# Layer 1's prologue written out on its own: decay and keys of batch 0 ahead of its gate, whose projection moves into the first period

## The reference

```
xa = layernorm(x); sx = previous row of xa - xa
t  = tanh((xa + sx * maa_x) @ maa_w1);  mw, mk, mv, mr, mg = t_f @ maa_w2[f]
x? = xa + sx * (maa_? + m?)                       for ? in w, k, v, r, g
w  = exp(-exp(time_decay + tanh(xw @ decay_w1) @ decay_w2))
r, k, v = xr @ Wr.T, xk @ Wk.T, xv @ Wv.T;   g = silu(xg @ Wg.T)
for each row l:  a = k_l v_l^T;  out_l = r_l (faaaa * a + s);  s = a + w_l * s
x = x + (groupnorm(out) * g) @ Wo.T;  then a gated feed-forward block on layernorm(x)
```

## Time and profile before

| what | us |
| --- | --- |
| median of 3 runs | 3539.14 |
| profiled execution, its time | 3535.91 |
| profiled execution, first to last instruction (span) | 3534.1 |
| layer 1, from its first instruction to its last unit, in the trace | 1400.87 to 2249.4 |
| first scan starts | 1470.82 |
| mean granted clock of TensorE, share of full | 0.968 |

### The profile page before, as it was taken

The page is one execution under the profiler, slowest core; times in us unless marked ns, Lnnn a source line. Parts: engine busy times, 40 slices in busy tenths (PEclk is TensorE's granted clock), DMA queues, the critical chain, the costliest instruction groups (busy, mean ns, idle before and its releaser), DMA issues. The chain is left out here.

```text
span 3534.1 us, 55156 instructions
## 1 busy us (share of the span) xinstructions
PE 3319.9 (94%) x21472; PEld 2547.0 (72%) x21472; DVE 2390.6 (68%) x3781; ACT 1787.9 (51%) x4255; POOL 196.2 (6%) x311
## 2 busy tenths in 40 slices
PE   7999999999999997889999998679999999699998
PEld 6777888887777785656666665357788788488885
DVE  6666666666665665499999999637777887642213
ACT  4555444444454443456565554427777777532222
POOL 0000000000000000000000000001111111000000
PEclk9999999999999999899999999879999999899999
DMA  5332212231122211544444444120001110210004
GB/s 215 124 105 107 108 72 76 97 115 72 72 96 90 78 73 57 156 114 103 111 108 102 114 103 108 41 108 3 35 31 70 44 48 31 88 53 24 24 12 162
DMA packets 93456, 296.08 MB, mean 84 GB/s; under 512 B 20016, under 2 KB 28208, under 8 KB 68752
## 3 DMA queue, kind: packets, MB, share of 16 engines
q1 hardware_dynamic: 64896, 186.47, 18.0%
q0 software_dynamic: 10368, 75.50, 5.6%
q10 hardware_dynamic: 17936, 30.59, 2.5%
HBM read 233.82 MB, written 58.72 MB: 83 GB/s over the span
## 5 line engine op out<-in xcount | busy, mean ns | idle before, releaser
L537 ACT ACTIVATE l_prob<-l_bank,l_nmax 128x512 f32<-128x512 f32 x512 | 345.3, 687 | 276.8 <-DVE l_nmax L679 276.8
L679 DVE TENSOR_REDUCE l_nmax<-l_bank 128x1 f32<-128x512 f32 x512 | 317.5, 682 | 71.4 <-PE l_bank L409 71.2
L375 PE MATMUL l_bank<-l_x_hi,l_w_hi 128*128 128x256 f32 x1024 | 298.0, 291 | 11.7 <-DVE l_x_lo L779 11.7
L702 DVE COPY l_probT<-l_bank 128x512 f32<-128x512 f32 x256 | 173.7, 689 | 175.3 <-PE l_bank L423 173.2
L375 PE MATMUL l_bank<-l_x_hi,l_w_lo 128*128 128x256 f32 x1024 | 290.9, 284 | 0.0
L375 PE MATMUL l_bank<-l_x_lo,l_w_hi 128*128 128x256 f32 x1024 | 290.7, 284 | 0.0
L1752 DVE TENSOR_TENSOR_SCAN l_kv<-l_wx,l_kv 128x2056 f32<-128x2056 f32 x64 | 283.8, 4434 | 1.6 <-DVE first_nrs L1765 1.2
L2320 ACT ACTIVATE l2a_sc<-l2a_sc,l2a_nmax 128x256 f32<-128x256 f32 x512 | 254.8, 508 | 41.1 <-DVE l2a_nmax L2436 41.1
L423 PE MATMUL l_bank<-l_ident,l_prob 128*128 128x128 f32 x2048 | 247.9, 275 | 10.7 <-DVE l_k_lo L695 6.3
L423 PEld LDWEIGHTS l_bank<-l_ident,l_prob 128*128 128x128 f32 x2048 | 225.8, 141 | 24.4 <-DVE l_k_lo L695 16.3
L445 PE MATMUL l_bank<-l_probT,l_v 128*64 128x512 f32 x1024 | 233.8, 598 | 0.0
(11 more groups left out here) (353 smaller groups left out, 8207.5 us busy)
## 6 DMA issues: line engine op xcount, KB each, us to landing
l_vb<-vd SPq DMA_DIRECT2D x64, 1024.0 KB
l_w_hi<-kept_w_hi POOLq DMA_DIRECT2D x24, 1024.0 KB, 8.2
l_w_lo<-kept_w_lo POOLq DMA_DIRECT2D x24, 1024.0 KB, 10.2
l_wv_hi<-kept_wv_hi POOLq DMA_DIRECT2D x12, 1024.0 KB, 5.1
l_wv_lo<-kept_wv_lo POOLq DMA_DIRECT2D x12, 1024.0 KB, 7.1
kept_w_hi<-l_w_hi SPq DMA_DIRECT2D x8, 1024.0 KB, 8.8
kept_w_lo<-l_w_lo SPq DMA_DIRECT2D x8, 1024.0 KB, 11.2
l2a_x<-x SPq DMA_DIRECT2D x16, 512.0 KB, 3.8
```

The source lines that it names most:

```text
L375: mm = pe.matmul(s.ap[:, c * ROWS:(c + 1) * ROWS], a[:, kt, c, g, :], b[:, kt, c * ROWS:(c + 1) * ROWS], start=m == 0, stop=m == 3 * KT - 1)
L537: act.activation(prob[h][:, it, :], s.ap[:, :], ACT.Exp, bias=nmax[:, n % 2, it, h:h + 1], accum_out=rsum[:, n % 2, it, h:h + 1]).then_inc ...
L679: dve.tensor_reduce(nmax[:, n % 2, it, h:h + 1], s.ap[:, :], AX.X, ALU.max, negate=True).then_inc(max_ready, 1)
L702: dve.tensor_copy(probT[0][:, j, :], s.ap[:, :]).then_inc(s.drained, 1)
```

## The change

The prologue is taken out of the loop (`ALL` is now `range(B + 1)`, POOL alone keeps its pass b = -1) and written out for each engine. Its order is new: mixtures v, w, g; centre_rows(1); project v; decay_in; mixture k; column_variances(1); decay_out; mixture r; project k half 0; spread_deviations(1); project r half 0. Project g of batch 0 stands in the first period, between centre_rows(2) and project v of batch 1. Inputs of batch 0 take other buffers: x, w, r in `xf[0]`, v and k in `xf[1]`, g in `ig[0]`. Since `xf[0]` now holds the input of r, `first_part(1)` waits until r half 1 of batch 0 is projected. `Wg` is loaded behind `Wk` and `Wr`.

```diff
@@ the list of PSUM tiles
-    ALL = range(-1, B + 1)
+    ALL = range(B + 1)
+    FIRST_INPUTS = ["x", "v", "w", "g", "k", "r"]
...
-    ring = []
+    ring = ["xT0_0", "xT0_1", "t0", "mv0_0", "mv0_1", "mw0_0", "mw0_1", "mg0_0", "mg0_1", "nc1_0", "nc1_1", "v0_0", "v0_1", "d0",
+            "mk0_0", "mk0_1", "nv1", "w0_0", "w0_1", "mr0_0", "mr0_1", "k0_0", "nr1", "r0_0"]
...
-        ring += [f"o{c}_0", f"o{c}_1"] if c is not None else []
+        ring += [f"o{c}_0", f"o{c}_1"] if c is not None else ["g0_0", "g0_1"]
...
+        def input_of(p, n):
...
+            if p == 0:
+                return {"x": xf[0], "v": xf[1], "w": xf[0], "g": ig[0], "k": xf[1], "r": xf[0]}[n]
+            return xf[INPUTS.index(n) % 2]
@@ SyncE
-                for n in ("Wv", "Wg"):
-                    sp.dma_start(W[n][:, :, :], d["l1_" + n]).then_inc(W_in[n], 16)
+                sp.dma_start(W["Wv"][:, :, :], d["l1_Wv"]).then_inc(W_in["Wv"], 16)
                 sp.dma_start(dw1[:, :, :], d["l1_dw1"]).then_inc(dw1_in, 16)
-                for n in ("Wk", "Wr"):
+                for n in ("Wk", "Wr", "Wg"):
@@ TensorE
+                turn("xT0", x)
+                pe.wait_ge(first_in, 32)
+                pe.wait_ge(w2_in, 48)
+                first(0)
+                mixture(0, "v")
+                mixture(0, "w")
+                mixture(0, "g")
+                centre_rows(1)
+                project(0, "v")
+                decay_in(0)
+                mixture(0, "k")
+                column_variances(1)
+                decay_out(0)
+                mixture(0, "r")
+                project(0, "k", (0,))
+                spread_deviations(1)
+                project(0, "r", (0,))
                 for b in ALL:
...
                         rows(f"o{c}", y, W["Wo"])
+                    else:
+                        project(0, "g")
                     if 0 <= p < B:
                         project(p, "v")
@@ ScalarE
                     if p:
                         full(act, S[f"k{p - 1}_1"])
+                    if p == 1:
+                        full(act, S["r0_1"])
...
+                turned(0)
+                first_part(0)
+                tanh(0)
+                mixture(0, "v")
+                mixture(0, "w")
+                mixture(0, "g")
+                centred(1)
+                for half in H2:
+                    project(0, "v", half, iv)
+                store_v(0)
+                decay_in(0)
+                mixture(0, "k")
+                decay_out(0)
+                mixture(0, "r")
+                project(0, "k", 0, ik)
+                start_state(0)
+                spread_w(0, 0)
+                stats(1)
                 for b in ALL:
...
                         spread_w(b, 2)
                     if c >= 0:
                         stats_c(c)
+                    else:
+                        full(act, S["g0_1"])
+                        for half in H2:
+                            project(0, "g", half, ig[0], ACT.Silu)
                     if now:
                         start_state(PER * b + 4)
@@ VectorE
+                shift(0)
+                first_input(0)
+                mix(0, "v")
+                mix(0, "w")
+                mix(0, "g")
+                column_deviations(1)
+                mix(0, "k")
+                mix(0, "r")
+                scale_rows(1)
+                spread(0)
                 for b in ALL:
```

More of the change, by code:

```diff
@@ L1025, in input_count @@
         def input_count(p, n):
-            return len(INPUTS) * p + INPUTS.index(n) + 1
+            return len(INPUTS) * p + (INPUTS if p else FIRST_INPUTS).index(n) + 1
+        def input_of(p, n):
+            if p == 0:
+                return {"x": xf[0], "v": xf[1], "w": xf[0], "g": ig[0], "k": xf[1], "r": xf[0]}[n]
+            return xf[INPUTS.index(n) % 2]
         def halves(ap):
@@ L1123, in _ @@
                 pool.memset(wx[:, :, 0], 0.0).then_inc(wx_zeroed, 1)
-                for b in ALL:
+                for b in range(-1, B + 1):
                     if b >= 1:
@@ L1219, in project @@
                     pe.wait_ge(xf_ready, input_count(p, n))
-                    columns(f"{n}{p}", W["W" + n], xf[INPUTS.index(n) % 2], own)
+                    columns(f"{n}{p}", W["W" + n], input_of(p, n), own)
                 def decay_in(p):
@@ L1228, in decay_in @@
                     for kt in range(CT):
-                        mm = pe.matmul(s.ap[0:64, 0:ROWS], dw1[:, kt, :], xf[1][:, kt, :], start=kt == 0, stop=kt == CT - 1)
+                        mm = pe.matmul(s.ap[0:64, 0:ROWS], dw1[:, kt, :], input_of(p, "w")[:, kt, :], start=kt == 0, stop=kt == CT - 1)
                     mm.then_inc(s.full, 1)
@@ L1302, in _ @@
                     if 0 <= p < B:
-                        if p:
-                            pe.wait_ge(xn_ready, p)
+                        pe.wait_ge(xn_ready, p)
                         turn(f"xT{p}", x)
@@ L1315, in _ @@
                     if 0 <= p < B:
-                        if p == 0:
-                            pe.wait_ge(first_in, 32)
-                            pe.wait_ge(w2_in, 48)
                         first(p)
@@ L1499, in mixture @@
                 def mixture(p, n):
-                    i = INPUTS.index(n)
+                    to = input_of(p, n)
                     if n == "v" and p:
                         full(act, S[f"r{p - 1}_1"])
-                    if n != "v":
+                    if n != "v" and p:
                         full(act, S[{"g": f"t{p}", "w": f"v{p}_1", "k": f"g{p}_1", "r": f"d{p}"}[n]])
+                    if n in "wkr" and p == 0:
+                        full(act, S[{"w": "t0", "k": "v0_1", "r": "d0"}[n]])
                     for half in H2:
@@ L1509, in mixture @@
                             m = M0 + MIX.index(n)
-                            ins = act.activation(xf[i % 2][:, ct, :], s.ap[:, ct % 2 * ROWS:(ct % 2 + 1) * ROWS], ACT.Identity,
+                            ins = act.activation(to[:, ct, :], s.ap[:, ct % 2 * ROWS:(ct % 2 + 1) * ROWS], ACT.Identity,
                                                  bias=vec[:, m, ct:ct + 1])
@@ L1792, in mix @@
                 def mix(p, n):
-                    i = INPUTS.index(n)
-                    to = xf[i % 2]
+                    to = input_of(p, n)
                     for half in H2:
@@ L1797, in mix @@
                     dve.tensor_tensor(to[:, :, :], to[:, :, :], sx[:, :, :], ALU.mult).then_inc(xf_part, 1)
-                    dve.wait_ge(xf_part, (len(INPUTS) - 1) * p + i)
+                    dve.wait_ge(xf_part, input_count(p, n) - 1 - p)
                     dve.tensor_tensor(to[:, :, :], to[:, :, :], xa[:, :, 1:ROWS + 1], ALU.add).then_inc(xf_ready, 1)
@@ L1895, in _ @@
                             gate_input(c)
-                        if 0 <= unit + 1 and b < B:
+                        if b < B:
                             spread(unit + 1)
```

## The result

| | before | after |
| --- | --- | --- |
| median, 20 runs each | 3536.15 us | 3548.59 us |
| lowest to highest | 3528.23 to 3546.00 | 3541.39 to 3554.56 |
| profiled execution's span | 3534.1 | 3549.3 |

The change makes the kernel slower: ratio 1.0031, 95% interval 1.0024 to 1.0038, 12.4 us by the medians. The forecast was 9.8 us. It named 3549 us and the median is 3548.59, but so near a hit is partly luck: its base, the median of 3 runs, was 3539.14, which is 3.0 above the median of 20.

The account below looks back on a forecast made before the run. The prediction took VectorE, 98% busy from the first unit on, to bound the kernel. To the median of 3539.14 us it added +1.0 (prologue) and +8.8 (first period), +9.8 in all, for 3549 us, range 3538 to 3558.

Parts of the forecast that it names:

- VectorE sets the pace behind the first unit: Layer 1, periods 1 to 8: VectorE is 98% busy, so each microsecond of earlier delay delays the kernel by one.
- The first scan hangs on x1_ready through SyncE's queue: End of prologue: the first value transfer, behind the store of x1, sets the first scan; it takes 14.68 us.
- Rival (b): First scan starts when keys and decay are ready, not held by x1_ready: -4.6 us, 3534.5; chance 0.05.
- Part 1: Prologue: TensorE's new order moves x1_ready and so the first scan by +1.0 us, bounds -1.4 and +4.0.
- Part 2: First period: first_part(1) on ScalarE waits for r half 1, so VectorE is 2.4 us late at first_input(1).
- Part 3: First period: project g delays the variances, VectorE waits 4.7 us, then again at scale_rows(2); +8.8 with Part 2.
- the second term: First period: VectorE's further wait at scale_rows(2), started at 1535.82, now 1544.64; 1.7 us.
- (a): First period: project g is hidden, only the wait of first_part(1) is paid: +3.4 us, 3542.5; chance 0.10.
- (c): Prologue and first period: 1.2 GHz over project k and project g or v: +14.5 us, 3553.6; chance 0.21.
- the bound of 10.6 us: Whole kernel: a change within 0.3%, 10.6 us, counts as no change; the forecast sum was just under it.

Follow-up runs that it names:

- a4: Changed kernel with SyncE's two first value loads ahead of store_x1(1) and load_att(2): 3534.55 us against 3537.05 for the kernel before, ratio 0.9992.
- b1: Kernel before with SyncE's two first value loads ahead of store_x1(1) and load_att(2): 3531.51 us, ratio 0.9985 to the kernel before.
- c1: Kernel before, unchanged, profiled once more: one execution, 3545.38 us.
- c3: Changed kernel, unchanged, profiled a second time: one execution, 3547.76 us.
- a2: Changed kernel with the input of r of batch 0 in tile y, so no wait of first_part(1): 3543.62 us, ratio 1.0016 to the kernel before.
- a3: Changed kernel with project g of batch 0 ahead of picks(0) and the input of r in y: 3538.27 us, ratio 0.9997 to the kernel before.
- a1: Changed kernel with project g of batch 0 moved into TensorE's idle time ahead of picks(0): 3541.86 us against 3539.19 before, ratio 1.0008.
- c2: Kernel before, unchanged, profiled a third time: one execution, 3545.84 us.
- a5: Changed kernel with project g of batch 0 ahead of picks(0), input of r in y, two value loads first: 3529.73 us, ratio 0.9984 to the kernel before.
- a7: Changed kernel with value loads first, input of r in y, project g of batch 0 ahead of picks(6): 3524.43 us against 3537.97 before, ratio 0.9961.
- b2: Kernel before with only the wait of first_part(1) for r half 1 of batch 0 added: 3543.92 us against 3537.05, ratio 1.0019.
- a6: Changed kernel with the 16 products of k half 1 of batch 0 done four times over: 3542.47 us, ratio 1.0013 to the kernel before.

## Why the prediction was right, and where its terms were off

**VectorE sets the pace behind the first unit: right.** Every delay of the first period was kept to the end of the layer: 681.8 us from unit 8 to the last scan against 680.9.

**The first scan hangs on x1_ready through SyncE's queue: right, and shown by a4 and b1.** Its transfer left 1.0 us behind scale_rows(1), as before. Rival (b), an early first scan, needed SyncE's order to change; with that order changed (a4) the gain is there.

**Part 1, +1.0: off.** In the pair of profiles it was +0.1 for x1_ready and -0.2 for the first spread. Two errors nearly cancel. From start to start decay_out took 1.99 us, mixture r 3.70 and half of k 4.99: by the prediction's own sum that is 1.99 + 3.70 + 4.99 - 8.79 = +1.89. Against it stands the mixture that moved ahead of project v, for which the prediction allowed some 2 us there. Before, mixtures v and g took 3.65 us together; after, v, w and g took 3.86. TensorE before, then after:

```profile
1419.84 1.99 PE L1212 MATMUL l_bank<-l_tT,l_w2a 32*128 32x256 f32 x8 [0.86 <-ACT l_tT L1495]
1421.67 1.88 PE L1212 MATMUL l_bank<-l_tT,l_w2b 32*128 32x256 f32 x8
```
```profile
1418.54 2.31 PE L1219 MATMUL l_bank<-l_tT,l_w2a 32*128 32x256 f32 x13 [0.86 <-ACT l_tT L1519]
...
1420.69 0.37 PE L1219 MATMUL l_bank<-l_tT,l_w2a 32*128 32x256 f32 x1
1420.81 0.37 PE L1219 MATMUL l_bank<-l_tT,l_w2b 32*128 32x256 f32 x1
```

Mixture w contracts rows 0 to 31 of its tiles, v and g rows 64 to 95. Products of w and g appear in turn, 0.11 us from start to start; products of one and the same mixture start 0.24 us apart. So mixture w came nearly free, 0.2 us for 1.9. Together that is +1.89 - 1.71 = +0.2, and spread_deviations(1) came 0.2 us later in the layer than before.

Against the five profiles of the old prologue the new one is some 3 us early (first spread at 67.0 to 68.9 in six profiles, 67.5 to 74.2 in four of the old). I had one profile, of an execution with little of the slow clock in its prologue. Read by half microseconds, the granted clock falls to 1.2 GHz at 20.6 us from the layer's start in the other four of the old prologue, during the first mixture, and is back at 27.5 (30.3 in c1). In the first profile of before and in all nine with the new prologue it stays at 2.4 GHz from 17.5 to 33 us. (My theory for c1, that the clock rises at one of two moments, is not what these rows show: it has risen by 17.5 us in all of them.) Up to the second mixture TensorE does the same in both prologues, so that their order of mixtures is not what keeps the clock up. Whether another part of the change does, or the nine had luck, is not settled.

**Part 2, the wait of first_part(1), 2.4: the mechanism right, its consequence left out.** The direct delay was 2.35 us at first_input(1), 2.5 counted from the first spread. Not forecast is what the wait does to TensorE: it sits idle 3.23 us behind r half 1, just after the clock had come back, and works at 1.2 GHz behind it, until VectorE waits for the bonus products (3.8 us, 2.4 in c3). Taking the wait away was worth 5 us with the gate in place (a2) and 0.11%, 4 us, without it (a3 against a1). I costed the wait on the engine that bounds and left out the engine whose clock it lets fall.

How much the gap costs is not one number. TensorE's stretch from the start of first(1) to the end of centre_rows(2) took, in all 14 profiles:

| ahead of first(1) | stretch, us | profiles |
| --- | --- | --- |
| idle 0.4 us or less | 15.1 | c1, c2, b1, a3 |
| idle 0.4 us or less | 16.7 to 16.8 | before, a2, a5, a7 |
| idle 3.23 us | 16.8 | b2, a4, a6 |
| idle 3.23 us | 18.4 | c3 |
| idle 3.23 us | 20.0 | after, a1 |

So 16.8, which the prediction took for granted from its one profile, already holds a slow spell (the line below, before), and behind a gap the stretch took 0 to 3.2 us more than that, or 1.7 to 4.9 us more than 15.1. In a6 the stretch is 16.8 where TensorE came out of its idle time at 2.4 GHz, but b2 came out of 10.65 us of idle time at 1.2 GHz and took 16.8 too. What decides between 16.8 and 20.0 is not shown.

```profile
1496.00:1500.00 4.00, 4.00 (x23) 2.51 (x23) 3.89 (x2) 1.02 (x4) 0.00 (x0) 0.57 0.51 119
```

The Trainium skill (TensorE: Matmul & The Clock Gate, "HAM oscillation — how this bites in real kernels") describes this: a wait that leaves TensorE idle lets the clock drop, and the work behind the gap is done slowly. The runs agree: behind the gap first(1)'s first eight products took 2.6 to 3.4 us in all six profiles that have it, and 1.9 to 2.0 in the eight without; and with idle time filled (a6) the kernel was 0.18% faster with more work. The page's other rule, which I weighed in the prediction, that activity releases the slow state, fails here once more: TensorE was busy 4.00 of 4.00 us in every stretch from 1500 to 1548, and this is one of them:

```profile
1532.00:1536.00 4.00, 4.00 (x10) 3.20 (x11) 3.97 (x4) 0.00 (x0) 0.00 (x0) 0.50 0.00 0
```

**Part 3, the gate ahead of the variances, 4.7 and 1.7: the mechanism right, the second term half of what came.** VectorE waited 3.93 us at the variances (3.71 in c3) and 3.63 at scale_rows(2) (0.37). Without the gate there (a1) the first wait goes and the second falls to 1.25, worth 8 us; without the r wait it is 0.19%, 7 us (a3 against a2). The part that scatters is scale_rows(2). From the end of the variances to spread_deviations(2) TensorE took 17.9 us before, 0.9 of it idle, and the forecast left 17.0. It took 18.6 us in four of the five profiles with the gate in that place (after, a2, a4, a6), and the wait was 3.63 in each; in c3 it took 15.3, with mixture w, the picks and project g of batch 1 all at full speed (7.17 us for the project, 9.21 in the first profile after).

**The rivals.** (a) fell: the waits came. (c), the clock, came true in size (+12.4 of its 14.5) by another way: project k was no slower than I took it and project g of batch 0 had the full clock; slow was the work ahead of that, first(1) to mixture g. Against this rival the prediction held that TensorE had full clock up to project v of the first period. That misread the trace of before, where the clock was 0.57 in 1496 to 1500 with TensorE busy 4.00 of 4.00 us. The rival got 0.21. With the forecast's own share past the bound of 10.6 us that made 0.43 for slower against 0.52 for no change. The medians are 12.4 us apart, past that bound, though the interval (1.0024 to 1.0038) holds values on both sides of it.

## What to carry to other kernels

Ask which queue releases the first unit before making its inputs earlier: here 11 us of earliness ended in a 15.44 us wait for a transfer that stood behind an unrelated store, and moving that store was worth 14 us in the changed kernel, while the reordering without it was worth nothing (a3). Work put into a busy engine's order must be held against the slack of the next result that the pacing engine takes from it (2.7 us for 7.1 us of work), and such a place must be looked for again each time the schedule around it moves (a5, a7). A new wait on one engine can also be a gap on TensorE: allow for the clock behind it, here 1.7 to 4.9 us behind a gap of 3.23, over a stretch with no slow spell.

## What the runs showed of the hardware

Doing the same 16 products four times over made the kernel some 6 us faster; in its profile TensorE came out of its idle time at 2.4 GHz. Mixtures that contract different rows overlap when they stand side by side: three took 3.86 us where two on the same rows took 3.65. With no edit at all, x1_ready in the old prologue stood at 51.8, 55.3 or 58.6 us from the layer's start in five profiles, by a slow spell of the granted clock between 20.6 and 30.3 us: a single profile's position is uncertain by more than most terms of such a sum.
